# Two-layer convolution and sparse-coding kernel: the odd set of tiles placed one search step behind the even one

## What is computed

```python
x = x + conv3x3(gn(x), ternary(w)) + sigmoid(gate) * conv3x3(gn(x), ternary(w_child))   # plus biases
x = x + omp(gn(x), dictionary)
```

## Time and profile before

| | us |
|---|---|
| median of three runs | 558.02 |
| lowest and highest run | 556.59, 558.44 |
| profiled execution, its own time | 555.17 |
| span of the profiled execution | 553.3 |
| VectorE busy in the span | 458.7 |
| TensorE busy in the span | 409.0 |
| ScalarE busy in the span | 309.3 |

### The profile page before, as it was taken

One profiled execution on the slowest core, in us unless ns is written; L12 is line 12 of the kernel. 1 busy time (PEld: TensorE's weight loads), 2 busy tenths in 40 slices (PEclk: granted clock), 3 DMA queues, 4 the chain that ended last, 5 costly groups with the idle time before them and its releaser, 6 DMA issues.

```text
span 553.3 us, 7423 instructions
## 1 busy us (share of the span) xinstructions
PE 409.0 (74%) x1666; PEld 296.3 (54%) x1666; DVE 458.7 (83%) x2325; ACT 309.3 (56%) x682; POOL 149.8 (27%) x162
## 2 busy tenths in 40 slices
PE   0099885899666669889893979998839557788674
PEld 0032772355556556456682854567738435676453
DVE  4483657878898979969999899989998999799990
ACT  2544436586656467668687385976802443465133
POOL 3000035334200063522300464433003644330010
PEclk9999996989878688989997979999978866899598
DMA  5979212789400025997510277613101754124155
GB/s 101 173 104 170 60 39 68 126 131 156 91 0 2 0 81 115 201 175 115 127 26 1 63 168 150 134 57 78 39 0 30 176 130 100 52 67 96 39 113 115
DMA packets 110202, 50.71 MB, mean 92 GB/s; under 512 B 103632, under 2 KB 104144, under 8 KB 110160
## 3 DMA queue, kind: packets, MB, share of 16 engines
q1 hardware_dynamic: 102000, 26.13, 28.9%
q0 software_dynamic: 8160, 24.13, 18.9%
HBM read 34.24 MB, written 8.65 MB: 78 GB/s over the span
## 4 chain that ended last, share of the span: by engine, by line
PE 43%; DVE 31%; ACT 8%; issue 6%; SPq 6%; DMA 5%; DVEq 0%; ACTq 0%
PE h L387 30%; PE conv_ps L387 10%; DVE junk L992 8%; DVE coef L1113 4%; DVE top L922 3%; DMA xb<-in_x 3%; SPq L248 3%; DVE top_i L935 3%; DVE top_i L937 2%; ACT score L636 2%; PE back_ps L387 2%; ACT diag L645 2%; ACT xb L602 2%; SPq L255 2%; DVE coef L1109 1%
## 5 line engine op out<-in xcount | busy, mean ns | idle before, releaser
L359 POOL DMA_INDIRECT rows<-gram,idx_u x128 | 131.5, 1027 | 346.7 <-DVEq L979 317.2
L387 PE MATMUL h<-rows,diag 128*128 128x256 f32 x640 | 165.9, 420 | 49.8 <-ACT diag L645 47.6
L387 PEld LDWEIGHTS h<-rows,diag 128*128 128x128 f32 x640 | 133.0, 212 | 83.6 <-issue 60.0
L645 ACT ACTIVATE diag<-ident,dx 128x128 f32<-128x128 f32 x320 | 96.8, 387 | 40.6 <-DVEq L1094 37.5
L992 DVE SCALAR_TENSOR_TENSOR junk<-mask,rows 128x256 bf16<-128x256 bf16 x320 | 119.4, 421 | 0.0
L636 ACT ACTIVATE score<-h 128x512 f32<-128x512 f32 x80 | 47.3, 597 | 99.4 <-PE h L387 99.0
L922 DVE MAX8 top<-score 128x8 f32<-128x256 f32 x160 | 65.3, 422 | 33.9 <-ACT score L636 32.3
L387 PE MATMUL h<-d_sb,z 128*128 128x256 f32 x256 | 66.6, 424 | 3.5 <-DVEq L913 2.5
L387 PE MATMUL back_ps<-coef_t,d_t 128*128 128x256 f32 x224 | 58.3, 419 | 13.3 <-ACT coef_t L651 13.3
L387 PEld LDWEIGHTS h<-d_sb,z 128*128 128x128 f32 x256 | 63.2, 330 | 6.9 <-issue 3.2
L387 PE MATMUL conv_ps<-xa,w_taps 128*64 128x512 f32 x128 | 61.7, 604 | 1.4 <-ACT x L614 1.0
(11 more groups left out here) (152 smaller groups left out, 506.0 us busy)
## 6 DMA issues: line engine op xcount, KB each, us to landing
xa<-in_x SPq DMA_DIRECT2D x64, 128.0 KB, 5.4
out<-x SPq DMA_DIRECT2D x64, 128.0 KB, 2.9
x<-y POOLq DMA_DIRECT2D x14, 512.0 KB, 4.7
xb<-in_x SPq DMA_DIRECT2D x42, 128.0 KB, 4.2
rows<-gram,idx_u POOLq DMA_INDIRECT x128, 3.1
xb<-in_x SPq DMA_DIRECT2D x14, 120.0 KB, 5.2
rows<-in_x SPq DMA_DIRECT2D x6, 128.0 KB, 4.4
d_sb<-in_L_conv_dictionary SPq DMA_DIRECT2D x4, 128.0 KB, 4.0
```

Of the source, the lines that this page charges most:

```text
L359: pool.indirect_dma_start(out=rows[s][:, k, t, :], out_offset=None, in_=gram_dram[:, :], in_offset=bass.IndirectOffsetOnAxis(ap=idx_u[s][: ...
L387: return nc.tensor.matmul(dst, lhs, rhs, start=start, stop=stop, skip_group_check=skip)
L645: last = nc.scalar.activation(diag[s][:, t, j, :], ident[:, :], ACT.Copy, scale=dx[s][:, k, t, j:j + 1])
```

## The change

**Order of the search.** VectorE now does (r,0,0), (r-1,1,4), (r,0,1), (r,1,0), (r,0,2), (r,1,1), (r,0,3), (r,1,2), (r,0,4), (r,1,3), and after the last round (3,1,4). The four `spread` calls of the round before follow steps (r,0,0) (two of them), the selection of (r,0,1), and (r,1,0). The `restart` of VectorE's counter falls away, and `h_read` is signalled at the end of `extract`.

**First group.** Sums, parameters and convolutions of round 0 go by pairs of images: pair 0 is normalized, convolved, normalized and correlated first, pair 1 beside step (0,0,0) and (0,0,1). SyncE loads the pair's `xa`, the dictionary and the pair's `xb` first. The weights, biases and the gate are loaded from ScalarE's queue. VectorE no longer normalizes images 1 to 3 of the first group (`apply_norm_x`); ScalarE does. VectorE still squares images 1 and 3, and normalizes y of images 0 to 2. `unread` gets a buffer of its own.

**Other engines.** Round 0 is written out on TensorE and ScalarE, and their `body` covers rounds 1 to 3 with convolution halves, reconstructions, evictions and statistics in new places. GpSimd's and SyncE's lists follow the new order. New on VectorE are `in_turn` (parts one after the other) and `pause` (a generator that yields without an instruction).

```diff
-    DVE_SQUARES = (1, 3)
     KEPT = 11
+    PAIRS = 2
+    STAGED = (STEPS - 1) * TILES * ATOMS
     BY_DMA = IMAGES - 2
...
-xb_first = rows[0][:, :, :, :].rearrange("p j t n -> p (j t n)")[:, 0:2 * GR * PAD_W].rearrange(
+xb_first = rows[1][:, :, :, :].rearrange("p j t n -> p (j t n)")[:, STAGED - 2 * GR * PAD_W:STAGED].rearrange(
...
-unread = three_images(z[:, 0:2, :].rearrange("p m n -> p (m n)"))
-unread_first = three_images(diag[1][:, :, :, :].rearrange("p t j n -> p (t j n)"))
+unread = sb("unread", [P, 3, GR + 1, W], BF16)
...
+def stage(f, p):
+    return p + 1 if f == 0 else f + PAIRS
+def images(f, p):
+    return slice(2 * p, 2 * p + 2) if f == 0 else slice(0, IMG_R)
+def sums_at(f, p, which, quantities):
+    width = images(f, p).stop - images(f, p).start
+    bank = p if f == 0 and which == 0 else 0
+    return conv_ps[:, bank, 0:quantities * width].rearrange("p (a m) -> p a m", m=width)
...
+    for m in range(2):
         load_a(m, m)
...
     d_view = dict_in.rearrange("(c r x) a -> r c (x a)", r=PATCH, x=PATCH)
     for q in range(PATCH):
         sp.dma_start(d_sb[q * C:(q + 1) * C, :, :].rearrange("p x a -> p (x a)"), d_view[q]).then_inc(d_loaded, 16)
...
-        load_b(m, b_part(0, m), xb_loaded[m] if m < 2 else xb_first_loaded[m - 2])
...
+    for m in range(2):
+        load_b(m, b_part(0, m), xb_loaded[m])
+    for m in range(2, IMG_R):
+        load_a(m, m)
+    for m in range(2, IMG_R):
+        load_b(m, b_part(0, m), xb_first_loaded[m - 2])
+    def load_ahead(f, m):
+        n = IMG_R * f + m
+        if f + 1 < ROUNDS or m + 2 < IMG_R:
+            sp.wait_ge(conv_done, 2 * n + 2)
+        if f == 0:
+            if m < 2:
+                load_b(n + IMG_R, xb[:, m], xb_loaded[m])
+        elif f + 1 < ROUNDS or m + 2 < IMG_R:
+            load_b(n + 2, xb[:, m % 2], xb_loaded[m % 2])
+        if f + 1 < ROUNDS:
+            load_a(n + IMG_R, m)
...
+    for m in range(2):
+        load_ahead(0, m)
     sp.wait_ge(gram_sb_done, 1)
     sp.dma_start(gram_dram.rearrange("(k p) a -> p k a", p=P), gram[:, :, :]).then_inc(gram_stored, 16)
...
+    for m in range(2, IMG_R):
+        load_ahead(0, m)
+    for r in range(ROUNDS):
+        if r > 1:
+            store(r - 2, 3)
+        for m in range(IMG_R):
+            if r + 1 < ROUNDS:
+                load_ahead(r + 1, m)
+            if r > 0 and m < 2:
+                store(r - 1, m)
+        if r > 0:
+            store(r - 1, 2)
+    store(ROUNDS - 2, 3)
...
+        gather(r, 0, 0)
+        if r > 1:
+            add_back(IMG_R * (r - 2) + 3)
+        gather(r, 0, 1)
+        if r > 0:
+            add_back(IMG_R * (r - 1))
+        gather(r, 1, 0)
+        gather(r, 0, 2)
+        if r > 0:
+            add_back(IMG_R * (r - 1) + 1)
+        gather(r, 1, 1)
+        gather(r, 0, 3)
+        gather(r, 1, 2)
+        gather(r, 1, 3)
+        if r > 0:
+            add_back(IMG_R * (r - 1) + 2)
+    add_back(IMG_R * (ROUNDS - 2) + 3)
...
+    def x_sums(f, p=0):
+        ms = images(f, p)
+        pe.wait_ge(x_stats, 2 * (IMG_R * f + ms.stop))
+        if f == 0 and p == 1:
+            pe.wait_ge(x1_done, 4)
+        mm(sums_at(f, p, 0, 2), same_channel[:, :], sum_x[:, :, ms], True, True).then_inc(x_stats_ps, 1)
...
+    def conv_half(f, m, b):
+        n = IMG_R * f + m
+        if b == 0:
+            pe.wait_ge(x_normed, n + 1)
+            if n == 0:
+                pe.wait_ge(x_normed_dve, 1)
+            pe.wait_ge(w_mid_ready, stage(f, m // 2))
+        if n > 0:
+            pe.wait_ge(x1_done, 2 * n - 1 + b)
...
+        last.then_inc(conv_done, 1)
     def conv(f, m):
...
+    conv(0, 0)
+    conv(0, 1)
     transpose_atoms()
...
     gram_matrix()
+    y_sums(0, 0)
+    x_sums(0, 1)
     correlate(0, 0)
+    pe.wait_ge(d_t_done, 1)
+    conv(0, 2)
+    conv(0, 3)
     pe.wait_ge(gram_sb_done, 1)
...
+    update(0, 0, 0)
+    y_sums(0, 1)
+    correlate(0, 1)
+    update(0, 0, 1)
+    update(0, 1, 0)
+    x_sums(1)
+    update(0, 0, 2)
+    conv(1, 0)
+    conv(1, 1)
+    update(0, 1, 1)
+    conv_half(1, 2, 0)
+    conv_half(1, 2, 1)
+    update(0, 0, 3)
+    conv(1, 3)
+    update(0, 1, 2)
+    y_sums(1)
+    correlate(1, 0)
+    def body(r, front):
         f = r + 1
         b = r - 1
...
+        if front:
+            x_sums(f)
+        if b > 0:
+            reconstruct(b - 1, 3)
+        update(b, 1, 3)
+        coef_transposes(b, 0)
+        update(r, 0, 0)
+        reconstruct(b, 0)
+        if front:
+            conv(f, 0)
         correlate(r, 1)
...
+        coef_transposes(b, 1)
+        reconstruct(b, 1)
+        update(r, 0, 1)
+        if front:
+            conv_half(f, 1, 0)
         update(r, 1, 0)
         if front:
...
+            conv_half(f, 1, 1)
+            conv_half(f, 2, 0)
+        update(r, 0, 2)
+        if front:
+            conv_half(f, 2, 1)
         update(r, 1, 1)
         if front:
...
+            conv_half(f, 3, 0)
+            conv_half(f, 3, 1)
+        update(r, 0, 3)
+        coef_transposes(b, 2)
+        if front:
+            y_sums(f)
         update(r, 1, 2)
...
+        reconstruct(b, 2)
         if front:
             correlate(f, 0)
...
+        coef_transposes(b, 3)
+    for r in range(1, ROUNDS):
+        body(r, r + 1 < ROUNDS)
+    reconstruct(ROUNDS - 2, 3)
+    update(ROUNDS - 1, 1, 3)
...
+    for i, (w_d, b_d) in enumerate([(w_in, b_in), (wc_in, bc_in)]):
+        act.dma_start(w_raw[:, i, :],
...
+    x_statistics(0, 0)
+    x_statistics(0, 1)
     act.wait_ge(d_loaded, 16 * PATCH)
     nc.scalar.activation(d_tmp[:, :, :], d_sb[:, :, :], ACT.Square).then_inc(d_sq, 1)
...
+    root(x_var, x_root, 0, 0, 0)
+    norm_x(0, 0)
+    norm_x(0, 1)
     act.wait_ge(d_nrm, 1)
     nc.scalar.activation(d_norm[:, 1, :], d_norm[:, 0, :], ACT.Sqrt).then_inc(d_root, 1)
...
+    out_conv(0, 0)
+    square_sum(0, 0)
+    x_statistics(0, 2)
+    out_conv(0, 1)
+    root(y_var, y_root, 1, 0, 0)
+    x_statistics(0, 3)
     act.wait_ge(d_t_ps, 1)
     for k in range(CHUNKS):
         last = nc.scalar.activation(d_t[:, k, :, :].rearrange("p c n -> p (c n)"),
                                     back_ps[k][:, :, :].rearrange("p a n -> p (a n)"), ACT.Copy)
     last.then_inc(d_t_done, 1)
...
+    root(x_var, x_root, 0, 0, 1)
+    norm_x(0, 2)
     scores(0, 0, 0)
...
+    norm_x(0, 3)
+    diags(0, 0, 0)
+    out_conv(0, 2)
+    square_sum(0, 2)
+    x_statistics(1, 0)
+    out_conv(0, 3)
+    scores(0, 0, 1)
+    root(y_var, y_root, 1, 0, 1)
+    x_statistics(1, 1)
+    norm_y(0, 3)
+    x_statistics(1, 2)
+    diags(0, 0, 1)
+    scores(0, 1, 0)
+    x_statistics(1, 3)
+    scores(0, 0, 2)
+    diags(0, 1, 0)
+    scores(0, 1, 1)
+    root(x_var, x_root, 0, 1)
+    norm_x(1, 0)
+    diags(0, 0, 2)
+    norm_x(1, 1)
+    scores(0, 0, 3)
+    out_conv(1, 0)
+    norm_x(1, 2)
+    square_sum(1, 0)
+    out_conv(1, 1)
+    diags(0, 1, 1)
+    norm_x(1, 3)
+    scores(0, 1, 2)
+    square_sum(1, 1)
+    out_conv(1, 2)
+    diags(0, 0, 3)
+    scores(0, 0, 4)
+    square_sum(1, 2)
+    out_conv(1, 3)
+    square_sum(1, 3)
+    diags(0, 1, 2)
+    scores(0, 1, 3)
+    root(y_var, y_root, 1, 1)
+    x_statistics(2, 0)
+    norm_y(1, 0)
+    norm_y(1, 1)
+    for m in range(1, IMG_R):
+        x_statistics(2, m)
+    scores(1, 0, 0)
+    def body(r, front):
         f = r + 1
         b = r - 1
...
+        norm_y(r, 2)
+        norm_y(r, 3)
+        if b > 0:
+            copy_coef(b - 1, 3)
+        diags(b, 1, 3)
         if front:
             root(x_var, x_root, 0, f)
         diags(r, 0, 0)
...
+        if b > 0:
+            out_back(b - 1, 3)
+        scores(b, 1, 4)
+        copy_coef(b, 0)
         if front:
             norm_x(f, 0)
         scores(r, 0, 1)
...
+        out_back(b, 0)
         if front:
             norm_x(f, 1)
+            out_conv(f, 0)
+        scores(r, 1, 0)
+        copy_coef(b, 1)
+        if front:
+            square_sum(f, 0)
+        diags(r, 0, 1)
+        out_back(b, 1)
+        scores(r, 0, 2)
+        if front:
+            norm_x(f, 2)
         diags(r, 1, 0)
...
         scores(r, 1, 1)
...
+        if front:
+            out_conv(f, 1)
+        diags(r, 0, 2)
+        if front:
+            norm_x(f, 3)
+            square_sum(f, 1)
+        scores(r, 0, 3)
+        if front:
+            out_conv(f, 2)
         diags(r, 1, 1)
...
         scores(r, 1, 2)
         if front:
...
+            square_sum(f, 2)
+        diags(r, 0, 3)
+        if front:
+            out_conv(f, 3)
+            square_sum(f, 3)
+        scores(r, 0, 4)
+        copy_coef(b, 2)
         diags(r, 1, 2)
         if front:
...
+            root(y_var, y_root, 1, f)
         scores(r, 1, 3)
...
         if front:
             norm_y(f, 0)
             norm_y(f, 1)
...
+        out_back(b, 2)
+        if f + 1 < ROUNDS:
+            for m in range(IMG_R):
+                x_statistics(f + 1, m)
+        if front:
             scores(f, 0, 0)
...
+    for r in range(1, ROUNDS):
```

(90 more changed lines are left out.)

347 lines of the change are left out of this document (72 added, 275 removed).

## The result

The changed kernel takes **603.45 us** (median of four runs, 602.44 to 604.28) against 557.31 (553.55 to 558.44) for the kernel before: a ratio of 1.084, 95% interval 1.0785 to 1.0895. The forecast was 564, with a range of 545 to 575. The direction was right, the size wrong by a factor of nearly eight (46.1 us where 6 were forecast).

A forecast was written before the change was run, and what follows sets the result against it. It took VectorE's work (busy 83% of the span) plus its waits, nearly all on ScalarE's scores, as the bound. Terms 0.8 + 7.6 + 1 - 3.6 = +5.8 us on 558.02 gave 564 us, range 545 to 575.

The forecast's parts named there:

- Up to (0,0,2): Start of round 0: 17.3 us gained at the first index, all spent again on pair 1; +0.8 us.
- (0,0,2) to (1,0,0): Rest of round 0: waits of 17.2 us against 9.6 before, +7.6 us, plus 1 us for chains running alone.
- the lone chains: Round 0: chains that run with nothing between their nine dependent instructions cost another 1 us.
- The 10 us before (0,1,2): Round 0, largest term: VectorE waits 10 us for scores, as ScalarE's norm_x(1,2) waits for the late reload of `xb`.
- x_sums: Round 0: VectorE waits 3 us for x_sums(1), which stands on TensorE behind update(0,1,0).
- Rounds 1 to 3: Odd steps cover even ones: 15 us of waits against 18.6 before, -3.6 us; bounds 6 and 22.
- The tail: Behind VectorE's last `spread`: the same work as before, 0 us.
- A cold TensorE: Rival: new idle stretches in round 0 put three pieces at half clock, 2.5 us each; 571 us; colder or later 0.15.
- The shifted set covers every wait: Rival: ScalarE catches up behind each odd step, decided at (0,1,2); 545 us, or 555 with reload waited for; faster 0.27.
- A warm TensorE: Rival: the shift fills idle stretches, so the clock rises, 1.5 to 2 us a round; 558 us; no change 0.11.
- The first group doesn't gain even 17 us: Rival: the start by pairs gains less than forecast; the same 571 us; colder or later 0.15.
- Its own signs: First index near 57; (0,0,2) at 91 to 95; 8 to 12 us before (0,1,2); 2 to 3 us before (r,0,3).

The follow-up runs named there:

- e7: Changed kernel with the loads of weights, biases and gate issued by SyncE ahead of the images, as in the kernel before; 600.94 us.
- e9: Changed kernel with the even set's updates of steps k = 2 and 3 cut to their newest index (8 passes for 24 and 32); 584.91 us.
- b3: Kernel before with the even set's updates of steps k = 2 and 3 cut to their newest index; 546.90 us, ratio 0.9860.
- e2: Changed kernel with norm_x(f,3) and square_sum(f,1) moved behind scores(r,0,3) in ScalarE's list, rounds 1 to 3; 602.16 us.
- e10: Changed kernel with the sets displaced in round 0 alone; rounds 1 to 3 in the order and lists of the kernel before; 588.75 us.
- e5: Changed kernel with 58 extra matmuls, results unused, on TensorE where it idles in round 0 and round 3; 596.50 us.
- e8: Changed kernel with the repairs of e2, e5 and e7 joined, and round 0 reordered on TensorE and ScalarE; 587.33 us.
- e11: e8 with the even set's updates of steps k = 2 and 3 cut to their newest index; 569.24 us.
- e1: Changed kernel with norm_x(1,2) and norm_x(1,3) moved behind scores(0,1,2) in ScalarE's list of round 0 alone; 603.33 us.
- b1: Kernel before with two norms (ScalarE) and two convolutions (TensorE) of the next group moved later, out_conv(f,3) left in place; 600.16 us.
- b2: Kernel before with extra matmuls, results unused, in TensorE's idle stretches, nothing else; 547.44 us, ratio 0.9884.

## Why the prediction was wrong, step by step

- **Up to (0,0,2): +0.8 forecast, +8.4 measured.** The idea held: the gain of pair 0 is spent on pair 1, with waits of 9.28, 7.49 and 2.98 us where 9, 6 and 2 were forecast. (As lateness of (0,0,2), which the forecast counted, it is 99.10 + 8.3 + 2.6 - 102.56 = 7.4.) Three terms were too small. The weights' loads cost 3.1 us where I wrote nothing (7.69 against 4.6, and e7 takes it back). The Trainium skill (DMA: Bandwidth & Descriptors, Issuing engines are not separate DMA queues) says that these DMAs interleave on the same engines whichever engine starts them; the trace agrees, and I wrote that they would land against the loads of x, but gave that no price. Correlation (0,0) took 9.37 us at a clock of 0.82 and (0,1) 9.93 at 0.75, where I had put 7.4 for both from a stretch at 1.00: 4.5 us together. The first index came at 60.78 and not at 56.8.
- **(0,0,2) to (1,0,0): +8.6 with the lone chains, +20.5 measured.** The 10 us before (0,1,2) were there: 12.76, with the ScalarE row that the prediction named (L652 waiting for the reload of `xb`). Too small were the wait at (0,0,3), 1.4 forecast and 2.27 + 1.50 measured, with its update at a clock of 0.72; that at (0,0,4), "covered", where 2.70 + 2.30 were measured; and that before (1,0,0), 2.5 forecast, 4.07 + 2.76 measured. Too large was x_sums, 3 against 1.0. (The four terms that the prediction names here add up to 16.9, not to its 17.2; and its rows of (0,0,0) land at 64.1 by its own terms, not at 64.6.)
- **Rounds 1 to 3: -3.6 forecast, +15.4 measured. This is the step that failed most.** "Here the idea holds" was wrong. I took 15 us of waits with 22 as the upper bound; they were 28.8. The rest of the 15.4 us is the second wait at (1,0,0), 2.8 us, which the forecast booked in round 0, and small gaps, 2.4. I priced each wait as ScalarE's list against VectorE's next step and gave "about 1 us" where the sum of diagonals, update and scores was near the length of the odd step between: 3.7 and 2.0 us were measured before (r,0,4) in rounds 1 and 2, and in round 3 3.2 before (3,0,3), where I had priced nothing, 4.4 before (3,0,4), where I had 1, and 5.3 at (3,1,4), where I had 0 to 1. Those odd steps, (r,1,1) and (r,1,2), are 8.3 and 9.9 us in the displaced order and 9.9 and 11.5 in the old one. e9 against b3 shows that about 10 us of the whole loss hang on the even updates' length, e2 that the norm before (r,0,3), for which 2.5 to 3 us were forecast and 3.3 and 5.3 measured, only passes its wait on, and e10 that rounds 1 to 3 in the old order take within 3 us their old time.
- **The tail: 0 forecast, 2.6 measured.** "The same work" was right, its clock was not: one multiplication took 6.28 us at 0.58 in place of 3.65 at 1.00, and in e5 the tail was 12.7 us long in place of 15.7 (13.1 before).
- **The rivals.** "A cold TensorE" had 0.15 and three places at 2.5 us each; e5 gave 6.9 us, near its 7.5, but it came on top of the others and not in place of them. "The shifted set covers every wait" is refuted: it decided at (0,1,2), where the scores came far too late. "A warm TensorE" is refuted for rounds 2 and 3 (0.91 and 0.80 against 0.92 and 0.83); round 1 rose from 0.91 to 0.93. "The first group doesn't gain even 17 us" came true in its condition (74.11 - 60.78 = 13.3 us), but the time went far beyond its 571.
- **Its own signs.** The wait before (0,1,2) with L652 behind the reload of `xb` is there; (0,0,2) came at 99.10, outside 91 to 95, and the waits before (r,0,3) were over 2 to 3 us. That the named largest term came true near its price does not save the sum.
- **The range** treated these as cases of which one would be true. They were terms of one sum with the same sign. e5 and e8 show that they add up; that each new wait itself lowered the clock for the next update is how I read the rows at 108.00 and 115.96, and it was not tried alone.

What stays open: e11 is 22 us above b3. By VectorE's idle time 4.0 of them lie before (0,0,2), 13.0 up to (1,0,0), 4.0 behind it up to VectorE's end and 1.5 in the tail. A wait of 8.2 us before (0,0,4) is the largest behind (0,0,2), and no run took it away.

## What to carry to other kernels

To displace one of two interleaved chains changes the cover of each of its links. Before the order of any list is drawn up, write for every step of one chain the length of what lies between it and its successor, against the whole latency of the link (here index, gather, diagonals, update and scores), at the clock that the trace shows for such stretches and not at the full one. A norm or convolution that stands before a released step should be moved on all engines or not at all: e1, which moved it in one list, passed the wait on; b1, which moved it in two but left one eviction behind, made waits of 16 us.

## What the runs showed that I had not expected

- Work without a use made the kernel before faster: b2 runs 163 more matmuls and takes 7.1 us less, 1.2% by the ratio, with the clock at 0.956 in place of 0.891. The Trainium skill (TensorE: Matmul & The Clock Gate, The HAM clock gate) puts the ramp penalty, for modeling, at under 1% of a typical kernel span. That speaks of a ramp, and here cold stretches come back all through the kernel (0.85, 0.85, 0.91, 0.92, 0.83 by stages); what covering some of them won is a little over that figure.
- The same update of 32 passes took 7.10 us at a granted clock of 1.00 and 8.75 at 0.81; a shorter one of 24 passes 5.40 at 1.00 and 7.53 at 0.72. The windows shown above tell them apart by what lies before: TensorE had worked 0.04 of the 8.00 us before 115.96, with the granted clock at 0.50 there, and 3.77 of the 5.90 us before 155.90, where it stayed at 1.00.
- The loads of weights and biases (two of 144 KB, two of 0.5 KB), issued by a second engine against the loads of x, landed 3.0 us later than when they stood first in one queue (w_sum's wait 7.69 against 4.7 in e7). The last of the four was issued at 3.2 us in both, so it is the landing that differs. e7 changed the engine and the place in the order at once; which of the two does it was not tried alone.
